# Compact 32x32 attention state on small tiles, its product in the bank of the FFN's second products, and one masking instruction over four banks

## The reference, cut to what matters

```python
q = relu(q * gate) ** 2 + EPS
k = relu(k * gate) ** 2 + EPS
def step(carry, inp):                       # over the positions
    kv_s = kv_s + k_t[..., :, None] * v_t[..., None, :]   # one 32x32 state per head
    k_s = k_s + k_t
    num = einsum('bhd,bhdm->bhm', q_t, kv_s)
    den = einsum('bhd,bhd->bh', q_t, k_s) + EPS
    return (kv_s, k_s), num / den
...
x = x + attention(...)
x = x + (gelu((LN(x) @ U1) @ V1 + b1) @ U2) @ V2 + b2
```

## Time and profile before

| | |
|---|---|
| median of 3 runs | 1833.25 us (1833.06 to 1835.95) |
| profiled execution, its own time | 1834.25 us |
| span of the profiled execution | 1831.9 us |
| granted TensorE clock, mean | 0.995 |
| PE busy | 1792.6 us (98%) |
| DVE busy | 1448.5 us (79%) |
| POOL busy | 798.7 us (44%) |
| ACT busy | 683.9 us (37%) |

### The profile page before, as it was taken

One profiled execution on the slowest core, in us unless ns is written; L12 is line 12 of the kernel. 1 busy time (PEld: TensorE's weight loads), 2 busy tenths in 40 slices (PEclk: granted clock), 3 DMA queues, 4 the chain that ended last, 5 costly groups with the idle time before them and its releaser, 6 DMA issues.

```text
span 1831.9 us, 34348 instructions
## 1 busy us (share of the span) xinstructions
PE 1792.6 (98%) x13753; PEld 1539.9 (84%) x13753; DVE 1448.5 (79%) x2606; ACT 683.9 (37%) x1242; POOL 798.7 (44%) x1027
## 2 busy tenths in 40 slices
PE   7899999999999999999999999999999999999997
PEld 4688888888888888888888888888888888888876
DVE  7777878878878878878878788778887788787775
ACT  4233343343333333333333433333433433333332
POOL 3253444444444444435434444434444444444430
PEclk9999999999999999999999999999999999999999
DMA  6001000001010011010011010011010010100000
GB/s 216 26 13 35 29 31 31 24 29 36 24 35 24 24 36 36 24 36 25 24 36 36 24 36 24 25 35 35 25 36 24 24 36 25 35 24 27 28 18 24
DMA packets 34508, 61.06 MB, mean 33 GB/s; under 512 B 3672, under 2 KB 6256, under 8 KB 34352
## 3 DMA queue, kind: packets, MB, share of 16 engines
q1 hardware_dynamic: 33488, 57.31, 9.6%
q10 hardware_dynamic: 864, 1.57, 0.2%
HBM read 41.96 MB, written 16.91 MB: 32 GB/s over the span
## 4 chain that ended last, share of the span: by engine, by line
PE 93%; DVE 1%; POOL 0%; ACT 0%; issue 0%
PE ps_a L786 9%; PE ps_a L784 9%; PE ps_a L785 9%; PE ps_t L791 6%; PE ps_b L786 6%; PE ps_b L785 6%; PE ps_b L784 6%; PE ps_q L784 4%; PE ps_b L984 3%; PE ps_h L784 3%; PE ps_h L785 3%; PE ps_h L786 3%; PE ps_q L785 3%; PE ps_q L786 3%; PE ps_c L962 3%; PE ps_c L974 3%
## 5 line engine op out<-in xcount | busy, mean ns | idle before, releaser
L378 POOL TENSOR_TENSOR h_lo<-h_full,h_hi 128x512 fp32r<-128x512 f32 x244 | 313.8, 1286 | 500.7 <-DVE h_hi L604 500.7
L459 ACT ACTIVATE h_full<-ps_h,cols 128x256 f32<-128x256 f32 x512 | 211.1, 472 | 243.7 <-PE ps_h L786 236.0
L604 DVE CAST h_hi<-h_full 128x512 fp32r<-128x512 f32 x256 | 176.2, 688 | 98.0 <-ACT h_full L459 97.8
L784 PE MATMUL ps_b<-wx_hi,zt_hi 128*128 128x512 f32 x512 | 206.9, 404 | 5.3 <-DVE key_sums L714 3.1
L784 PE MATMUL ps_a<-wx_hi,zt_hi 128*128 128x512 f32 x512 | 208.2, 407 | 0.0
L786 PE MATMUL ps_b<-wx_hi,zt_lo 128*128 128x512 f32 x512 | 203.3, 397 | 0.0
L785 PE MATMUL ps_b<-wx_lo,zt_hi 128*128 128x512 f32 x512 | 203.2, 397 | 0.0
L786 PE MATMUL ps_a<-wx_hi,zt_lo 128*128 128x512 f32 x512 | 202.3, 395 | 0.0
L785 PE MATMUL ps_a<-wx_lo,zt_hi 128*128 128x512 f32 x512 | 201.8, 394 | 0.0
L340 POOL TENSOR_TENSOR small<-moments,eps_col 128x1 f32<-128x1 f32 x128 | 25.8, 201 | 391.5 <-DVE moments L753 327.1
L784 PE MATMUL ps_q<-h_hi,u_hi 128*128 128x256 f32 x512 | 159.5, 311 | 7.3 <-DVE h_lo L609 5.1
(11 more groups left out here) (173 smaller groups left out, 5053.0 us busy)
## 6 DMA issues: line engine op xcount, KB each, us to landing
xs<-L_attn_x SPq DMA_DIRECT2D x64, 256.0 KB, 2.8
out<-x1s SPq DMA_DIRECT2D x64, 256.0 KB, 2.1
key_sums<-carry_rows SPq DMA_DIRECT2D x60, 256.0 KB, 3.2
x1s<-L_attn_W_gate SPq DMA_DIRECT2D x4, 256.0 KB, 4.0
x1s<-L_ffn_U SPq DMA_DIRECT2D x4, 256.0 KB, 3.8
carry_rows<-key_sums SPq DMA_DIRECT2D x64, 2.0 KB
probs<-L_attn_W_qkv SPq DMA_DIRECT2D x3, 256.0 KB, 6.0
bias<-L_attn_b_qkv ACTq DMA_DIRECT2D x3, 256.0 KB, 6.8
```

What stands on the lines that cost most here:

```text
L378: E.tensor_tensor(h_lo[:, i % 2, :], h_full[:, i % 2, :], h_hi[:, i % 2, :].bitcast(F32), ALU.subtract).then_inc(s["h_lo_ready"], 1)
L459: last = E.activation(h_full[:, i % 2, a * GROUP:(a + 1) * GROUP], ps_h[i % 2][:, a * GROUP:(a + 1) * GROUP], ACT.Gelu_apprx_tanh, bias=b1 ...
L604: E.tensor_copy(h_hi[:, i % 2, :], h_full[:, i % 2, :]).then_inc(s["h_hi_ready"], 1)
L784: E.matmul(ps, wh, mh, start=start and i == 0, stop=False)
```

## The change

**State.** `state_bd` (128 x 4 x 4 x 128) becomes `state` (128 x 4 x 4 x 32): only the 32x32 blocks are kept, head j of a group on partitions 32j to 32j+31. The readout becomes 16 matmuls, each on one 32x32 tile of the array on the diagonal, with 128 moving columns as before. The state product becomes 16 matmuls on 128x32 tiles with 32 moving columns each.

**Place.** The state product now writes to `ps_q`, columns 256 to 383 or 384 to 511 by the parity of the chunk, beside the accumulating q product. On PE it moves behind q pair 1, directly ahead of the output product, and no longer waits for a mask. A new wait stands ahead of q pair 2: the state must have been added by DVE.

**Masks.** The four score banks become one PSUM tensor of four neighbouring banks, and one DVE instruction over 2048 columns replaces the four. All waits on `probs_ready` count one instead of four. The four adds to the state become one of 128 partitions x 128 elements.

```diff
-        state_bd = sb("state_bd", [P, 4, KT, P])
+        state = sb("state", [P, 4, KT, HEAD])
...
-        ps_a = bank("ps_a")
+        scores = ctx.enter_context(nc.psum_tensor("scores", [P, HPG * DM], F32))
+        ps_c, ps_d, ps_t, ps_a = (scores[:, j * DM:(j + 1) * DM] for j in range(HPG))
         ps_b = bank("ps_b")
-        ps_t = bank("ps_t")
-        ps_c = bank("ps_c")
-        ps_d = bank("ps_d")
...
+        def state_cols(c):
+            return ps_q[:, GROUP + c.half * KT * HEAD:GROUP + (c.half + 1) * KT * HEAD]
...
-            E.memset(state_bd[:, :, :, :].rearrange("p b k n -> p (b k n)"), 0.0).then_inc(s["state_zero"], 1)
+            E.memset(state[:, :, :, :].rearrange("p b k n -> p (b k n)"), 0.0).then_inc(s["state_zero"], 1)
...
                     dve.wait_ge(s["scores_done"], c.done())
-                    for j in range(HPG):
-                        E.tensor_tensor(probs[:, j, :].rearrange("p (k t) -> p k t", k=KT),
-                                        ps_scores[j][:, :].rearrange("p (k t) -> p k t", k=KT),
-                                        causal.unsqueeze(1).broadcast_to([P, KT, P]), ALU.mult)\
-                            .then_inc(s["probs_ready"], 1)
+                    blocks = HPG * KT
+                    E.tensor_tensor(probs[:, :, :].rearrange("p j (k t) -> p (j k) t", k=KT),
+                                    scores[:, :].rearrange("p (g t) -> p g t", g=blocks),
+                                    causal.unsqueeze(1).broadcast_to([P, blocks, P]), ALU.mult)\
+                        .then_inc(s["probs_ready"], 1)
                     if ffn.exists:
                         h_head(ffn, pairs[2], finishing)
                     dve.wait_ge(s["state_done"], c.done())
-                    for j in range(HPG):
-                        q = slice(HEAD * j, HEAD * (j + 1))
-                        mine = state_bd[q, c.slot, :, q]
-                        new = ps_c[:, :].rearrange("p (k n) -> p k n", k=KT)[q, :, q]
-                        last = E.tensor_tensor(mine, new, mine, ALU.add)
-                    last.then_inc(s["state_ready"], 1)
+                    mine = state[:, c.slot, :, :].rearrange(flat)
+                    E.tensor_tensor(mine, state_cols(c), mine, ALU.add).then_inc(s["state_ready"], 1)
...
                         for ft in range(KT):
-                            E.matmul(ps_b[:, ft * P:(ft + 1) * P], state_bd[:, c.slot, ft, :],
-                                     query_t[:, ft, :], start=ft == 0, stop=False, skip_group_check=True)
+                            for j in range(HPG):
+                                rows = slice(HEAD * j, HEAD * (j + 1))
+                                E.matmul(ps_b[rows, ft * P:(ft + 1) * P], state[rows, c.slot, ft, :],
+                                         query_t[rows, ft, :], start=ft == 0, stop=False,
+                                         tile_position=(HEAD * j, HEAD * j), skip_group_check=True)
...
                 if ffn.exists:
                     q_pair(ffn, pairs[0])
                     h_pair(ffn, pairs[2])
-                if c.exists:
-                    pe.wait_ge(s["value_ready"], c.done())
-                    pe.wait_ge(s["probs_ready"], c.done(HPG, 1))
-                    for ft in range(KT):
-                        cols = slice(ft * P, (ft + 1) * P)
-                        mm = E.matmul(ps_c[:, cols], keys[:, c.half, cols], values[:, c.half, cols],
-                                      start=True, stop=True)
-                    mm.then_inc(s["state_done"], 1)
                 if ffn.exists:
                     q_pair(ffn, pairs[1])
                 if c.exists:
-                    pe.wait_ge(s["probs_ready"], c.done(HPG, HPG))
+                    pe.wait_ge(s["value_ready"], c.done())
+                    for ft in range(KT):
+                        for j in range(HPG):
+                            cols = slice(ft * P + HEAD * j, ft * P + HEAD * (j + 1))
+                            mm = E.matmul(state_cols(c)[HEAD * j:HEAD * (j + 1), ft * HEAD:(ft + 1) * HEAD],
+                                          keys[:, c.half, cols], values[:, c.half, cols],
+                                          start=not ffn.exists and ft == 0, stop=True,
+                                          tile_position=(0, HEAD * j), skip_group_check=True)
+                    mm.then_inc(s["state_done"], 1)
+                    pe.wait_ge(s["probs_ready"], c.done())
...
                 if ffn.exists:
                     h_pair(ffn, pairs[3])
+                    if c.exists:
+                        pe.wait_ge(s["state_ready"], c.done())
                     q_pair(ffn, pairs[2])
```

More of the change, by code:

```diff
@@ L817, in tz @@
                 if before.exists:
-                    pe.wait_ge(s["probs_ready"], before.done(HPG, HPG))
+                    pe.wait_ge(s["probs_ready"], before.done())
                 transpose4(zs, s["tz_done"])
@@ L868, in step @@
                     else:
-                        pe.wait_ge(s["probs_ready"], d.done(HPG, HPG))
+                        pe.wait_ge(s["probs_ready"], d.done())
                     transpose4(queries, s["tq_done"])
@@ L894, in step @@
                         if a:
-                            pe.wait_ge(s["probs_ready"], before.done(HPG, 2))
+                            pe.wait_ge(s["probs_ready"], before.done())
                         else:
```

## The result

The changed kernel takes 1839.17 us (median of 13 runs, 1834.61 to 1840.69) against 1833.25 us (13 runs, 1832.1 to 1835.95): ratio 1.0026, 95% interval 1.0018 to 1.0035. It is slower by a quarter of a per cent where 1.8 us less was forecast. The profiled execution took 1839.17 us, its span is 1837.1 us, 5.2 more than before.

What follows compares the result with a forecast made beforehand. PE, 98% busy, was taken as level with a chain ending in POOL at q pair 2. 29 x 0.02 + 30 x 0 + 2 x 0.4 + 2 x 0.2 = 1.8 us less, median 1831.4; range 1826.5 to 1839.5.

Steps and rivals of the forecast that it cites:

- The absorbing chain: At q pair 2, POOL's `h_lo` stays fixed, so PE's saving becomes a wait: gain 0.02 even, 0 odd.
- Sizes of the parts: Per-step values: readout +0.1, state product 0.3 instead of 0.90, one mask 2.3 instead of 2.49 us.
- by the starts: Lower estimate of the single mask on DVE, from four mask starts 0.60 apart: 2.2 us.
- the new wait ahead of q pair 2 ... holds none of them: State wait met at cast + 0.3, `h_lo` at cast + 1.36, so q pair 2, key sums and y are not held.
- the two first chunks have no FFN, and the output product follows the mask: 0.2 each: At the start, the shorter mask lets the output product come earlier: gain 2 x 0.2 us.
- The end: In the last odd step and last chunk PE is really behind, so its saving counts: 2 x 0.4 us.
- rivals 2 and 3: Slower: small state product costs as much as output product, 1838.7, chance 0.09; odd cast misses its turn behind `key_lo`, 1839, 0.06.
- the odd cast: DVE's cast of pair 2 in odd steps, asking 0.23 before POOL's bias add ends, goes ahead of `key_lo`.
- Rival 4: Readout: diagonal tiles don't run side by side, 3.5 us instead of 0.98, +126 us, 1958; chance 0.05.

Runs made afterwards that it cites:

- e7: e1 with PE making the state product a second time, result unused, in every step with FFN work; 1836.46 us, ratio 1.0005.
- e8: e4 with the state product made a second time, result unused, in every step with FFN work; 1825.14 us, ratio 0.9953.
- e4: e1 with POOL's bias add on xs moved from ahead of `key_lo` to behind `h_lo` of pair 2; 1808.02 us, ratio 0.9852.
- e5: Kernel before with only POOL's bias add on xs moved behind `h_lo` of pair 2; 1830.31 us, ratio 0.9984.
- e1: Changed kernel with the wait for the added state moved from ahead of q pair 2 to ahead of h pair 3; 1835.21 us, ratio 1.0000.
- e2: Kernel before with one added wait for the state of the same chunk ahead of q pair 2; 1837.82 us, ratio 1.0016.

## Why the prediction was wrong, point by point

- **The absorbing chain: right.** PE and the chain through POOL are level at q pair 2, and what PE saves there becomes a wait. The wait came out at 0.45 in the even step (917.05 + 0.12 to 917.62) and 0.58 in the odd (946.28 + 0.12 to 946.98). The forecast gives 0.37 (912.58 to 912.95) and 0.49 (941.75 to 942.24); the rest is the new 0.09. e7, e8, e4 and e5 show it from four sides.
- **Sizes of the parts: right.** Readout +0.11 (1.01 against 0.98, and 0.20 instead of 0.12 from the last matmul of h pair 1), 0.1 forecast. State product 0.27, 0.3 forecast. Mask 2.29, 2.3 forecast; its lower end of 2.2 "by the starts" does not follow, since four starts 0.60 apart make 2.4, and in the odd step the readout's 0.1 was left out of the mask's end (939.23, not 939.13, still ahead of 939.26). Neither enters the sum. State add 0.28. State and output product together 1.31, some 1.2 forecast. DVE's busy time fell by 112 us where 75 were forecast, of which the masks (27.6) and the adds (54.8) are 82; the rest is open, and DVE does not hold the step.
- **The step that failed first: "the new wait ahead of q pair 2 ... holds none of them".** It was priced by when its semaphore is met, cast + 0.3 against `h_lo` at cast + 1.36, which is so. But a met wait is not free where it stands beside the late one: +0.09 from `h_lo` to q pair 2, +3.7 us in the regular steps where -0.6 was forecast. e1 took it away, e2 made it alone.
- **The step that failed second: "the two first chunks have no FFN, and the output product follows the mask: 0.2 each".** The mask does end earlier: in the second of these chunks the output product starts 3.58 behind the first score instead of 3.78, the 0.2 of the forecast. The sum took that for the whole effect and put the clock at nothing. The state product, though, had split the gap while the mask ran, and moving it ahead left PE idle for 2.0 us in one piece; in the profiled execution the clock stood at 1.2 GHz for 6.8 us twice. +2.9 us where -0.4 was forecast, 0.55 of them before the first scores and of open cause.
- **The end: right in sign, undersized.** 1.4 us won, 0.8 forecast.
- **The rivals.** The result lies at the time of rivals 2 and 3, and neither is its cause: the state product is small, and the odd cast keeps its turn (0.55). The stated range reached to 1839.5 for the sake of these rivals; that 1839.17 falls inside it is luck. The Trainium skill's 60 cycles a matmul (TensorEngine Tiling, Instruction Overhead), 0.8 us as an estimate from the page, don't hold for column tiles side by side: 32 records took 0.27 us, and the measurement decides. Rival 4 is out: the diagonal tiles run four abreast.

## What to carry to other kernels

When an engine is 98% busy, look at the one wait in its stretch that another chain meets at the same moment: adding work there, as e7_double does, tells in one run whether a saving can count. A wait that is met long before still has a price if it is put next to the wait that is met last; put it an instruction group earlier. And before moving work out of a gap, ask what the gap does to the clock.

## What the runs showed of the hardware that was not expected

- Two waits ahead of one weight load, the last one met late: 0.14 to 0.15 us from the releaser's end to the matmul (after, e2_bwait), 0.05 with one wait (before, e1_early).
- 16 fp32 matmuls on 128x32 tiles with 32 moving columns, 32 records, take 0.27 us beside others of their shape, 8.4 ns a record.
- One 2.0 us gap of PE, after a stretch with smaller gaps, was followed by 6.8 us at 1.2 GHz in the profiled executions of after and e1_early and by none in that of e7_double, with the same program up to there.
